# Masked attention over a sparse adjacency on one Trainium2 core: lists over 16 groups of 256 columns instead of 8 of 512

## The reference

```python
q = x @ Wq.T + bq;  k = key @ Wk.T + bk;  v = value @ Wv.T + bv
scores = (q @ k.T) / 64
s = scores * adj
s = where(abs(s) < 1e-5, -1e9, s)
out = layernorm(x + (softmax(s) @ v) @ Wm.T + bm)
```

## Time and profile before

| | |
|---|---|
| median of 3 runs | 486.85 us (486.71 to 488.02) |
| profiled execution, span first to last instruction | 484.0 us (only its span is given; the median is 2.85 us above it) |
| PE busy | 449.9 us, 93% |
| DVE busy | 329.2 us, 68% |
| POOL busy | 256.5 us, 53% (its DMA issuing counts here as rows of 1.0 us) |
| ACT busy | 214.3 us, 44% |
| front, to the first `scores` | 188.6 us |
| loop, from there | 295.4 us |

### The profile page before, as it was taken

One profiled execution on the slowest core, in us unless ns is written; L12 is line 12 of the kernel. 1 busy time (PEld: TensorE's weight loads), 2 busy tenths in 40 slices (PEclk: granted clock), 3 DMA queues, 4 the chain that ended last, 5 costly groups with the idle time before them and its releaser, 6 DMA issues.

```text
span 484.0 us, 5751 instructions
## 1 busy us (share of the span) xinstructions
PE 449.9 (93%) x1556; PEld 247.0 (51%) x1556; DVE 329.2 (68%) x907; ACT 214.3 (44%) x471; POOL 256.5 (53%) x258
## 2 busy tenths in 40 slices
PE   6999999999999958999998999999889999999882
PEld 2444444444443424666555666655556565656641
DVE  0155544499625961989898789898886889564774
ACT  1223422243333122443654645646536546547585
POOL 3100000300582004787787777778777777777740
PEclk9999999999999988999999999999999999999996
DMA  8999999889999995899999668999996695765753
GB/s 319 374 213 230 281 293 237 148 222 266 294 269 303 242 288 163 219 243 296 262 280 330 207 218 273 241 281 335 278 336 213 188 291 154 234 195 165 228 170 114
DMA packets 42037, 119.74 MB, mean 247 GB/s; under 512 B 7109, under 2 KB 11973, under 8 KB 40978
## 3 DMA queue, kind: packets, MB, share of 16 engines
q0 software_dynamic: 19008, 70.59, 59.0%
q1 hardware_dynamic: 15842, 28.92, 16.6%
q10 hardware_dynamic: 7152, 19.83, 11.1%
HBM read 140.62 MB, written 17.83 MB: 327 GB/s over the span
## 4 chain that ended last, share of the span: by engine, by line
PE 49%; DMA 15%; DVE 11%; POOL 11%; issue 8%; ACT 5%; POOLq 0%; DVEq 0%; ACTq 0%
PE bank L550 12%; PE bank L541 11%; DMA key_g<-key,index 6%; PE bank L666 6%; PE bank L686 6%; DMA big<-xT 5%; POOL key_g L430 4%; PE bank L584 3%; PE bank L646 3%; DMA big<-adj_tiles 3%; POOL v_g L441 3%; PE bank L598 3%; POOL adj_g L452 3%; PE bank L607 1%; POOL big L421 1%
## 5 line engine op out<-in xcount | busy, mean ns | idle before, releaser
L550 PE MATMUL bank<-big,M 128*128 128x456 f32 x288 | 123.8, 557 | 7.4 <-DMA big<-xT 7.4
L541 PE MATMUL bank<-y_buf,big 128*128 128x512 f32 x256 | 111.2, 594 | 0.0
L441 POOL DMA_INDIRECT v_g<-table,index x72 | 77.7, 1079 | 36.2 <-issue 21.0
L430 POOL DMA_INDIRECT key_g<-key,index x72 | 77.1, 1070 | 27.1 <-issue 20.7
L452 POOL DMA_INDIRECT adj_g<-adj_cols,index x72 | 73.9, 1027 | 21.9 <-issue 18.9
L421 POOL DMA_DIRECT2D big<-adj_tiles x36 | 20.6, 574 | 121.9 <-PE bank L541 69.8
L989 DVE TENSOR_TENSOR big<-big 128x1824 bf16<-128x1824 bf16 x36 | 39.6, 1099 | 60.4 <-DMA big<-adj_tiles 60.4
L541 PEld LDWEIGHTS bank<-y_buf,big 128*128 128x128 f32 x256 | 48.2, 190 | 59.6 <-issue 59.6
L550 PEld LDWEIGHTS bank<-big,M 128*128 128x128 f32 x288 | 50.6, 194 | 40.0 <-issue 37.7
L666 PE MATMUL bank<-keyT,qT 128*114 128x256 f32 x288 | 68.5, 381 | 0.8 <-ACT keyT L860 0.5
L686 PE MATMUL bank<-v_g,probT 128*114 128x512 f32 x140 | 65.8, 592 | 0.0
(11 more groups left out here) (117 smaller groups left out, 529.7 us busy)
## 6 DMA issues: line engine op xcount, KB each, us to landing
big<-adj_tiles POOLq DMA_DIRECT2D x36, 912.0 KB, 10.1
x_buf<-x SPq DMA_DIRECT2D x36, 256.0 KB, 4.7
out<-y_buf SPq DMA_DIRECT2D x35, 256.0 KB, 4.0
big<-valueT ACTq DMA_DIRECT2D x8, 1024.0 KB, 9.9
big<-xT SPq DMA_DIRECT2D x7, 912.0 KB, 11.3
table<-qT ACTq DMA_DIRECT2D x5, 1024.0 KB, 20.2
table<-y_buf ACTq DMA_DIRECT2D x3, 1024.0 KB, 18.6
big<-xT ACTq DMA_DIRECT2D x2, 912.0 KB, 19.7
```

Source lines behind the costliest of these rows:

```text
L430: pool.indirect_dma_start(key_g[:, b, c, :], None, key, bass.IndirectOffsetOnAxis(index[:, t, c:c + 1], 0), bounds_check=N - 1, oob_is_err ...
L441: pool.indirect_dma_start(v_g[:, b, c, :], None, table, bass.IndirectOffsetOnAxis(index[:, t, c:c + 1], 0), bounds_check=N - 1, oob_is_err ...
L541: mm = nc.tensor.matmul(bank[4 + t % 2][:, :], col_buf[nb % 2][:, d, k * P:(k + 1) * P], G[:, d, :], start=(d == 0), stop=(d == DC - 1))
L550: mm = nc.tensor.matmul(ps[:, 0:QR], M[:, d, a * P:(a + 1) * P], col_buf[nb % 2][:, d, 0:QR], start=(d == 0), stop=(d == DC - 1))
```

## The change

The number of groups (`G8` = 8, now `NG` = 16) doubles, so a cell covers 256 columns; the batches are 8, 8, 8, 8 and 4 tiles; a list holds 32 (four passes). 18 trees stand in front and 18 in the loop, by another table, and the list steps stand elsewhere. A list now takes five iterations in the loop instead of six. In front, batch 0 and batch 1 are listed after fewer trees, and `value_sums` stands behind the trees.

```diff
-G8 = 8
-GK = N // G8
+NG = 16
+GK = N // NG
-BATCH = (9, 9, 12, 6)
-START = (0, 9, 18, 30)
+BATCH = (8, 8, 8, 8, 4)
+START = (0, 8, 16, 24, 32)
-LIST = 48
+LIST = 32
...
-        FIRST = 20
-        TREES = {i: [FIRST + i] for i in range(10)} | {i: [FIRST + i - 5] for i in range(15, 21)}
-        LIST_AT = {2: 10, 3: 21}
-        COUNTS = 27
+        FIRST = 18
+        TREES = ({0: [FIRST, FIRST + 1]} | {i: [FIRST + i + 1] for i in range(1, 8)}
+                 | {i: [FIRST + i - 2] for i in range(11, 16)} | {i: [FIRST + i - 6] for i in range(20, 24)})
+        LIST_AT = {2: 7, 3: 15, 4: 23}
+        STEPS = 5
+        COUNTS = 28
...
             pool.wait_ge(index_ready, 2 * CH)
-            for t, units in ((16, 23), (17, 25), (18, 27), (19, 29)):
+            for t, units in ((16, 23), (17, 25)):
                 gather_keys(t - 16)
                 gather_adj(t - 16)
                 pool.wait_ge(v_ps, units)
                 load_adj(t)
+            for t in range(2, KD):
+                gather_keys(t)
+                gather_adj(t)
             for i in range(3):
                 for t in trees_of(i):
                     load_adj(t)
...
             for t in range(3 * DC, UNITS):
                 value_rows(t)
-                if t == 14:
+                if t == 13:
                     pe.wait_ge(prep_sb, 2 * DC + 1)
                     lists(0)
-                if t == 16:
+                if t == 15:
                     sum_counts(0)
-                if t == 20:
+                if t == 18:
                     pe.wait_ge(prep_sb, 2 * DC)
                     spread_slots(0)
+                if t == 27:
+                    lists(1)
                 if t == 30:
-                    lists(1)
+                    sum_counts(1)
...
-                if t == 10:
+                if t == 9:
                     bias_columns()
                     number(0)
...
-                if t == 13:
+                if t == 11:
                     index_slots(0)
                 if t == START[2] - 1:
                     number(1)
                     count(1)
                     for k in range(PASSES):
                         take_8(1, k)
-                    value_sums()
                     shift_bits(1)
                     shift_lists(1, 0, SHIFTS)
+            value_sums()
...
-                if step in (1, 2):
-                    take_8(b, 2 * step - 1)
-                    take_8(b, 2 * step)
-                if step == 3:
-                    take_8(b, PASSES - 1)
-                    shift_bits(b)
-                    shift_lists(b, 0, 2)
-                if step == 4:
-                    shift_lists(b, 2, SHIFTS)
+                if step == 1:
+                    for k in range(1, PASSES):
+                        take_8(b, k)
+                if step == 2:
+                    shift_bits(b)
+                    shift_lists(b, 0, 4)
+                if step == 3:
+                    shift_lists(b, 4, SHIFTS)
```

More of the change, by code:

```diff
@@ L25 @@
 SLOTS = CH * P
-GS = SLOTS // G8
-SPC = P // G8
+GS = SLOTS // NG
+SPC = P // NG
 MAXR = -(-GK // GS)
@@ L30 @@
 QBL = T // 4
-BATCH = (9, 9, 12, 6)
-START = (0, 9, 18, 30)
+BATCH = (8, 8, 8, 8, 4)
+START = (0, 8, 16, 24, 32)
 LB = len(BATCH)
 BT = max(BATCH)
-CELLS = BT * G8
-LIST = 48
+CELLS = BT * NG
+LIST = 32
 PASSES = LIST // 8
@@ L107, in build @@
         big = sb("big", [P, T * D])
-        AW = R * K4 * G8
-        H1, H2, H3, H4 = (n * K4 * G8 for n in (57, 29, 15, 8))
+        AW = R * K4 * NG
+        H1, H2, H3, H4 = (n * K4 * NG for n in (57, 29, 15, 8))
         adj_buf = [big[:, i * 1824:(i + 1) * 1824].bitcast(BF16) for i in range(AB)]
@@ L115, in build @@
         t4 = big[:, 13008:13136].bitcast(BF16)
-        lw = big[0:CELLS, 13136:13648]
+        lw = big[0:CELLS, 13136:13136 + GK]
         c_prod = big[0:P, 13648:14160]
@@ L324, in list_step @@
             for b, at in LIST_AT.items():
-                if at <= i <= at + 5:
+                if at <= i < at + STEPS:
                     return b, i - at
@@ L555, in lists @@
             def lists(b):
-                n = BATCH[b] * G8
+                n = BATCH[b] * NG
                 pe.wait_ge(any_sb, START[b] + BATCH[b])
@@ L574, in spread_slots @@
                 pe.wait_ge(shifted, (b + 1) * (2 * SHIFTS))
-                n, cells = BATCH[b], BATCH[b] * G8
+                n, cells = BATCH[b], BATCH[b] * NG
                 for c in range(CH):
@@ L717, in _ @@
                     sum_counts(b)
-                if step == 5:
+                if step == STEPS - 1:
                     spread_slots(b)
@@ L737, in _ @@
                             n = BATCH[b]
-                            nc.tensor.matmul(bank[6][:, (b * CH + c) * BT:(b * CH + c) * BT + n], g_spread[0:n * G8, c, :],
-                                             tile_select[0:n * G8, 0:n], start=True, stop=True).then_inc(g_spread_ps, 1)
+                            nc.tensor.matmul(bank[6][:, (b * CH + c) * BT:(b * CH + c) * BT + n], g_spread[0:n * NG, c, :],
+                                             tile_select[0:n * NG, 0:n], start=True, stop=True).then_inc(g_spread_ps, 1)
                     wait_apart(pe, g_index, r * (2 * CH * LB) + 2 * CH * LB)
@@ L1002, in cells_of @@
             def cells_of(b):
-                return slice(0, BATCH[b] * G8)
+                return slice(0, BATCH[b] * NG)
             def number(b):
@@ L1008, in number @@
                 dve.wait_ge(list_ps, b + 1)
-                nc.vector.scalar_tensor_tensor(left[c, b, :], list_bank(b)[c, :], 0.0, descending[c, :],
+                nc.vector.scalar_tensor_tensor(left[c, b, :], list_bank(b)[c, 0:GK], 0.0, descending[c, :],
                                                ALU.is_gt, ALU.mult).then_inc(left_sb, 1)
@@ L1407, in layout @@
     const[:, C_ID:C_ID + P] = np.eye(P)
[L1408 to L1411 removed]
+    const[:, C_DESC:C_DESC + GK] = NG * (GK - np.arange(GK))[None, :] - (p % NG)[:, None]
+    const[:, C_GRP:C_GRP + P] = (p % NG)[:, None] == (p // SPC)[None, :]
+    const[:, C_SEL:C_SEL + BT] = (p // NG)[:, None] == np.arange(BT)[None, :]
     i = np.arange(CELLS)
[L1413 removed]
+    const[:, C_SUMS:C_SUMS + CELLS] = ((p // NG)[:, None] == (i // NG)[None, :]) & (p[:, None] < i[None, :])
     const[:, C_BIT:C_BIT + SHIFTS] = (1 << np.arange(SHIFTS, dtype=np.int32)).view(np.float32)
```

22 lines of the change are left out of this document (8 added, 14 removed).

## The result

| | before | after |
|---|---|---|
| median | 487.02 us (486.71 to 488.02) | 496.18 us (494.37 to 496.75) |
| ratio | | 1.0177 (95% interval 1.0149 to 1.0204) |
| profiled execution | span 484.0 us | span 493.9 us, its time 495.68 us |

What follows compares the result with a forecast made beforehand. PE was busy 93% of the span, with DVE pacing the tree iterations. Terms -4.6 + 3.1 + 2.3 - 6.4 - 2.0 + 8.4 + 3.0 = +3.8 us on span 484.0 give 487.8, plus 2.85 makes 490.6; range 486.2 to 493.5.

Steps and rivals of the forecast that it cites:

- Late second x^T: End of the front: with tile 22's load moved away, x^T lands at 177.0 us; front -4.6 us, clock included.
- the rival of the early x^T: Front: x^T lands before PE asks for it, so the front gains 8.1 us instead of 4.6; 487.1 us, chance 0.08.
- The step that failed in front: POOL's queue in front, ahead of tile 22's load: same tiles and key gathers in nearly the same order, so nothing changes.
- Two trees, +3.1: Iteration 0: DVE is the pace from iteration 1 on, so the second tree arrives whole, +3.1 us.
- The list step on a tree, +2.3: Iteration 7: a list step on top of a tree, on DVE's pace, +2.3 us (bounds 2.0 and 3.4).
- Late keys, -6.4: Loop: PE's five waits for keys that POOL gathered late go, and 0.1 behind each, -6.4 us.
- The step that failed in the loop: Remaining list steps: short enough for what iterations without a tree leave DVE, -2.0 us (0 to -3).
- The waits in 15 and 23, +8.4: Iterations 15 and 23: PE's list transposes wait for the same iteration's tree, 4.2 us twice, +8.4 (6.2 to 8.6).
- the clock, +3.0: Behind the waits in iterations 15 and 23: PE's clock falls, 1.5 us each, +3.0 (0 to 4.4).
- The steady clock: Rival: 4.2 us waits don't lower PE's clock and the front's gap costs it nothing; 486.5 us, chance 0.15.
- POOL as the true pace: Rival, in the loop: PE only follows POOL, so its waits at 15 and 23 are given back; 481.8 us, chance 0.09.
- The late x^T: Rival, in the front: x^T is as late as before, so the -4.6 us is gone; 495.2 us, chance 0.10.

Runs made afterwards that it cites:

- e4_before_load22: Kernel before, with only the adjacency load of tile 22 moved behind the gathers of values: 481.72 us, ratio 0.9868.
- e3_pool_order: Changed kernel, with the adjacency load of tile 18 ahead of the gather of tile 3's keys again, as before the change: 496.92 us, ratio 1.0188.
- e1_trees_early: Changed kernel, with the trees of tiles 27 to 31 and 32 to 35 one iteration earlier: 488.97 us, ratio 1.0022 to the kernel before.
- e2_fill_wait: Changed kernel, with four dummy PE matmuls ahead of the waiting list transposes in iterations 15 and 23: 491.8 us, ratio 1.0086.
- e5_lists_later: Changed kernel, with its three list steps in the loop one iteration later (8, 16, 24 instead of 7, 15, 23): 485.15 us, ratio 0.9948.
- e7_counts27: Changed kernel, with the counts of lists read in iteration 27 instead of 28, as before the change: 497.31 us, ratio 1.0178.
- e8_one_tree: Changed kernel, with its nine trees at the loop's start spread one to an iteration over 0 to 8: 497.28 us, ratio 1.0209.
- e10_after_combined: Changed kernel, with list steps at 7, 16 and 24 and the adjacency loads of tiles 18 to 21 in quarters: 480.33 us, ratio 0.9848.
- e9_half_loads: Changed kernel, with the adjacency loads of tiles 18 and 19 issued in halves (packets of 3648 bytes): 493.42 us, ratio 1.0103.
- e6_quarter_loads: Changed kernel, with the adjacency loads of tiles 18 and 19 issued in quarters (packets of 1824 instead of 7296 bytes): 490.52 us, ratio 1.0052.

## Why the prediction was right in sign and too small

**Late second x^T: the mechanism held.** e4_before_load22 shows the load of tile 22 responsible (-6.4 us by the ratio, of which the traces show 3.3, where 4.6 was charged). In the changed kernel the second x^T landed 17.6 us behind ACT's issue, at 175.5, instead of 23.6 us behind it, and the second wait went wholly: 8.1 us, as the rival of the early x^T had it.

**The step that failed in front** is "Unchanged before that: the same seven tiles and four key gathers stand in that queue in nearly the same order". They do, and POOL's queue even moved the same 3.2 MB while the first x^T was on its way; but that x^T took 2 us longer all the same. The first wait grew by 2.4 us and brought the clock down for another 2.3: 4.7 us that the sum put at nothing. The halves and quarters show by dose that the loads' long packets set how long x^T takes; that the gathers' earlier place is what lengthened it is not shown, e3_pool_order speaks against it, and the stores in ACT's queue are a rival. It is luck that the front came out near the forecast (3.5 net, not 4.6): two misses, +4.7 and -3.5, nearly cancel. A further 1.4 us had been lost before ACT's issue of x^T. No cause was found for it, and it may be the spread of executions: the same issue stands between 142.44 and 143.73 in e1, e2, e3, e5, e7, e8 and the changed kernel, whose fronts are alike but for POOL's order in e3, and at 142.33 and 142.87 in the kernel before and e4.

**Two trees, +3.1:** measured +3.0, of which 2.5 in iteration 1. DVE's `soften` comes every 8.1 us from iteration 1 on, as read; PE's iterations 1 to 3 still took 7.81 before and feel it from iteration 4 on. e8_one_tree shows that the same 3 us come wherever the ninth tree stands. **The list step on a tree, +2.3:** +2.0; DVE's rows of the step last from 254.48 to 256.88, 2.4 us. (By the rows that it names, half the width saves 0.74 - 0.43 = 0.31 and not 0.28, which makes the term 2.2.)

**Late keys, -6.4:** -5.5. They went as said. e10_after_combined shows them to be the shadow of a fast PE: with PE 15 us faster they are back.

**The step that failed in the loop** is "stay within what an iteration without a tree leaves DVE", the remaining list steps at -2.0. The stretches outside the other terms got 0.3 us longer; their iterations from 10 to 30 took 5.0 us over 7.81 each before and 5.5 now, where about 4 was counted on. What I had booked as list steps was in part not theirs: every fourth iteration takes some 0.4 us over 7.81 in both kernels (10, 14, 22 and 30 before, 10, 18, 22 and 26 after, all 8.2 to 8.3), and 30 before and 22 after have no list step. And one step got dearer: the counts, moved to iteration 28, put `count_rounds` (1.3 us) on DVE behind `scales`, which waits for ACT:

```profile
446.98 0.18 DVE L1232 RECIPROCAL rstd<-std 114x4 f32<-114x4 f32 x1 [4.32 <-ACT std L895]
447.19 0.16 DVE L1234 SCALAR_TENSOR_TENSOR shift<-mean_var,rstd 114x4 f32<-114x4 f32 x1
447.27 0.47 DVE L1097 TENSOR_REDUCE small<-bank 1x1 f32<-1x128 f32 x2
```

Iteration 30 takes 9.41 us for it. With 2.3 us this is the largest net miss of the sum, though a change of one digit in the diff showed a part of it. The 0.9 of e7_counts27 is the part that was tested; the rest is read from the first rows of the iterations.

**The waits in 15 and 23, +8.4, and the clock, +3.0: right.** The idle times are 4.13 and 4.09 us, forecast 4.2; the stretch got 12.2 us longer against 11.4. e1_trees_early and e5_lists_later take the waits away, e2_fill_wait the clock alone. The Trainium skill's price (TensorE: Matmul & The Clock Gate, under its terms) is half of the time at the lower clock. The clock was low for 3.4 us around 322 and for 6.8 around 393, so by the price the two cost 5.1 us, an estimate. The trace doesn't agree, e2_fill_wait gave back 3.7. If only what lies behind the end of each wait counts, some 2.9 and 4.9 us, the same half makes 3.9.

**Rivals.** The steady clock is refuted by the windows. POOL as the true pace is refuted too: iterations 15 and 23 kept what they lost, and PE waited for no keys at all. The late x^T (495.2) came near the time but not by its mechanism: the second x^T was early. The early x^T came true for the second wait, and its gain went into the first.

The miss of 6.1 us on the span is then: counts and list steps 2.3, the start 1.4, the front 1.1, keys 0.9, waits and clock 0.8, less 0.4 for the two DVE terms.

## What to carry to other kernels

When a loop table is changed, list for each iteration everything that one engine has to do in it, and look for the iterations with two entries: nearly every variant here paid where a tree and a list step met, and most shifts of one only moved the meeting. In these runs a transfer on the path was delayed by the length of the packets in the other queue and not by its bytes alone, so try to cut bulk loads beside it into pieces; here that was worth some 4 us in the front. And if a change also moves something small in a queue, try that part alone: moving one load was worth 1.3%, and the rest of the change cost more than that.

## What the runs showed of the hardware

**Gaps of equal length, different clock.** Nine traces have the double tree in iteration 1, and PE waits 2.23 to 2.34 us there. In seven of them the clock stays at 1.00 behind the gap, in e9_half_loads (2.28) and e10_after_combined (2.23) it falls to 0.50, and iteration 1 takes 11.96 and 11.38 us instead of 10.3. The gap of e6_quarter_loads ends at the same 196.76 us as that of e9_half_loads and is as long, 2.28; behind it the windows view has, for e6 and then for e9:

```profile
198.00:200.00 2.00, 2.00 (x9) 1.42 (x8) 1.90 (x4) 0.64 (x1) 1.70 (x3) 1.00 1.04 355
198.00:200.00 2.00, 2.00 (x4) 0.92 (x3) 1.90 (x4) 0.00 (x0) 1.69 (x3) 0.50 1.01 299
```

Iteration 8 is alike: 2.27 us left the clock up in the changed kernel and brought it down in e3_pool_order (10.38 and 10.87 us). All gaps of 3.9 us and more had a fall in them or right behind them; the 1.51 in front did not. So in this kernel a gap of some 2.3 us may go either way at the same place of the same program, its length does not decide it, and what does was not settled.

**The same wait, different loss.** Behind the wait of 4.13 us iterations 15 and 16 took 21.6 us in the changed kernel, 23.2 in e7_counts27 and 22.8 in e8_one_tree (there the wait was 4.08), with no difference in the program around them.

**Shorter packets cost no bandwidth here.** From 150 to 156 us the two queues moved 1.50 MB with packets of 7296 bytes on POOL's side, 1.50 MB with halves and 1.62 MB with quarters.
